# Reading q's and k's parts for attention as three runs each, twelve transfers a group in place of 18

## The reference

```python
h = _modulate(_ln(x), sh_msa, sc_msa)
qkv = (h @ w_qkv + b_qkv).reshape(B, N, 3, nh, hd).transpose(2, 0, 3, 1, 4)
q, k, v = (qkv[0], qkv[1], qkv[2])
attn = jax.nn.softmax(jnp.einsum('bhqd,bhkd->bhqk', q, k) * hd ** (-0.5), axis=-1)
o = jnp.einsum('bhqk,bhkd->bhqd', attn, v).transpose(0, 2, 1, 3).reshape(B, N, C)
x = x + g_msa[:, None, :] * (o @ w_proj + b_proj)
xn = _modulate(_ln(x), sh_mlp, sc_mlp)
x = x + g_mlp[:, None, :] * mlp(xn)
```

## Time and profile before

| | |
|---|---|
| median of three runs | 1612.34 us |
| the profiled execution: its time | 1615.5 us |
| the profiled execution: its span | 1613.7 us, 41194 instructions |
| TensorE matmuls busy | 1441.4 us, 89% |
| TensorE loads busy | 1082.4 us, 67% |
| VectorE busy | 1039.2 us, 64% |
| ScalarE busy | 780.9 us, 48% |
| GpSimd busy | 543.7 us, 34% |
| SyncE's transfers | 129.75 MB, 37.0% of 16 engines' span |

### The profile page before, as it was taken

How to read it: one execution, slowest core, us unless ns; L and a number is a source line. 1 busy time by engine, 2 the same in 40 slices (tenths; PEclk the granted TensorE clock), 3 DMA queues, 4 the chain that set the end, 5 groups by cost and what they waited for, 6 DMA issues and landing times. The chain is left out here.

```text
span 1613.7 us, 41194 instructions
## 1 busy us (share of the span) xinstructions
PE 1441.4 (89%) x15976; PEld 1082.4 (67%) x15976; DVE 1039.2 (64%) x2592; ACT 780.9 (48%) x1287; POOL 543.7 (34%) x739
## 2 busy tenths in 40 slices
PE   6789988999999998988999678787999798988998
PEld 2467666777777775766777467665776576666776
DVE  4678875666767666878447688886445565655342
ACT  2367654333323326766545366664544354645443
POOL 3345532211131303544334224433334243432321
PEclk9799999999999998999999789999999799988999
DMA  4765631111122214555011433443208576785021
GB/s 129 147 148 141 153 85 51 49 42 42 34 75 60 59 42 96 135 125 121 17 30 45 105 88 90 116 108 82 43 23 111 85 100 112 117 118 98 11 67 45
DMA packets 210858, 134.95 MB, mean 84 GB/s; under 512 B 144189, under 2 KB 193048, under 8 KB 204458
## 3 DMA queue, kind: packets, MB, share of 16 engines
q1 hardware_dynamic: 190706, 129.75, 37.0%
q10 hardware_dynamic: 19960, 2.57, 1.3%
HBM read 98.24 MB, written 33.24 MB: 81 GB/s over the span
## 5 line engine op out<-in xcount | busy, mean ns | idle before, releaser
L1532 DVE TENSOR_REDUCE negm<-banks 128x8 bf16<-128x1024 f32 x256 | 311.4, 1216 | 110.8 <-PE banks L650 108.4
L1223 ACT ACTIVATE prob<-banks 128x1024 f32<-128x1024 f32 x256 | 262.2, 1024 | 244.9 <-PE banks L672 244.2
L1949 POOL TENSOR_TENSOR X<-X,gx 128x288 f32<-128x288 f32 x128 | 104.9, 832 | 303.6 <-DVE gx L1562 301.7
L1350 ACT ACTIVATE hid<-banks 128x512 f32<-128x512 f32 x144 | 85.9, 597 | 230.5 <-PE banks L951 230.5
L650 PE MATMUL banks<-qk 54*128 54x128 bf16 (+1 forms) x2048 | 125.3, 245 | 65.5 <-DVE negm L1532 22.0
L668 PE MATMUL banks<-qk 54*128 54x128 bf16 (+1 forms) x2048 | 173.3, 239 | 8.6 <-ACT prob L1223 5.0
L967 PEld LDWEIGHTS banks<-wfc,hid 128*128 128x128 f32 x1152 | 156.6, 190 | 29.9 <-issue 19.9
L672 PE MATMUL banks<-mT,identb 64*128 64x128 bf16 x2048 | 170.2, 229 | 2.1 <-issue 2.1
L967 PE MATMUL banks<-wfc,hid 128*128 128x144 f32 x1152 | 161.1, 286 | 0.0
L950 PE MATMUL banks<-hT,wfc 128*128 128x512 f32 x288 | 149.4, 600 | 1.6 <-DMA wfc<-in_L_cond_w 1.1
L684 PE MATMUL banks<-prob,V 128*32 128x128 f32 x4096 | 150.5, 292 | 0.0
(11 more groups left out here) (165 smaller groups left out, 2822.8 us busy)
## 6 DMA issues: line engine op xcount, KB each, us to landing
qk<-qk_scr SPq DMA_DIRECT2D x336, 72.0 KB
gbuf<-gate_scr SPq DMA_DIRECT2D x64, 288.0 KB, 4.5
qk_scr<-parts SPq DMA_DIRECT2D x48, 288.0 KB, 3.0
qk<-qk_scr SPq DMA_DIRECT2D x48, 216.0 KB
qk<-cw_scr SPq DMA_DIRECT2D x8, 1024.0 KB, 4.6
qk<-tok_scr SPq DMA_DIRECT2D x112, 72.0 KB
qk_scr<-parts SPq DMA_DIRECT2D x48, 144.0 KB, 2.8
qk<-qk_scr SPq DMA_DIRECT2D x48, 144.0 KB
```

The lines of the kernel that those rows point to most:

```text
L1223: act.activation(prob[:, 2 * (U % 3):2 * (U % 3) + 2, :], pairs[1][:], ACT.Exp, scale=scale).then_inc(a_exp, 1)
L1532: dve.tensor_reduce(negm[:, u // 2, :, 4 * (u % 2):4 * (u % 2) + 4], pairs[0][:].rearrange("q s (h k) -> q s h k", k=T), AX.X, ALU.max, ne ...
L1949: pool.tensor_tensor(x, x, gx[:, q, :, :], ALU.add).then_inc(g_x, 1)
```

## The change

The six products are the same, in another order. q's blocks become 0, 1 | 0, 1, 2 | 0 and k's 0, 1, 2 | 0 | 0, 1, which pair as 00, 11, 02, 10, 20, 01. Each side is thus three runs of consecutive parts, and a run is one transfer: 18, 27 and 9 rows for q, and 27, 9 and 18 rows for k. `read_parts` issues 2 halves x 2 sides x 3 runs = 12 transfers a group in place of 18, in all four layers; `fetched` counts 96 for each third group. The rows, the bytes, the row lengths, the order of halves, the waits ahead of them and everything else stay as they are.

```diff
--- before.py
+++ after.py
@@ -26,6 +26,8 @@
 REM = 4 * CR_CH + 2
 QK_ROWS = 96
 QK_DIMS = QK_ROWS // H
+
+RUNS = (((0, 2), (0, 3), (0, 1)), ((0, 3), (0, 1), (0, 2)))
 KS = 6 * D
 TB = T // H
 TOK_V = [96, 48]
@@ -283,7 +285,7 @@
             return 64 * (n + 1) if n < 24 else 64 * 24 + 192 * (n + 1 - 24)
 
         def fetched(n):
-            return 144 * (n // 3 + 1)
+            return 96 * (n // 3 + 1)
 
         def normal(k):
 
@@ -430,22 +432,18 @@
                     sp.wait_ge(d_hg, CR + NT * (1 if n == 8 else 8))
                 sp.wait_ge(q_w, written(n))
                 for s in range(2):
-                    r0 = 64 * s
-                    for part in range(3):
-                        rows = (3 - part) * D
-                        if l < 3:
-                            q_src, k_src = (qk_scr[p, side, :, :, 8 * s:8 * s + 8].rearrange("a d h t -> (a d) (h t)")
-                                            for side in range(2))
-                            q_dst = qq[r0:r0 + rows, r].rearrange("r h t -> r (h t)")
-                            k_dst = kk[r0:r0 + rows, r].rearrange("r h t -> r (h t)")
-                        else:
-                            q_src, k_src = (tok_scr[p, side, 2 * s:2 * s + 2].rearrange("c b a d h w -> (a d) (c b) (h w)")
-                                            for side in range(2))
-                            q_dst, k_dst = qq[r0:r0 + rows, r], kk[r0:r0 + rows, r]
-                        sp.dma_start(q_dst, q_src[0:rows]).then_inc(q_r[r][s], 16)
-                        for i in range(3 - part):
-                            sp.dma_start(k_dst[D * i:D * i + D], k_src[D * part:D * part + D]).then_inc(q_r[r][s], 16)
-                        r0 += rows
+                    for side, runs in enumerate(RUNS):
+                        row = 64 * s
+                        for first, many in runs:
+                            if l < 3:
+                                src = qk_scr[p, side, first:first + many, :, 8 * s:8 * s + 8].rearrange("a d h t -> (a d) (h t)")
+                                dst = qk[row:row + many * D, side, r].rearrange("r h t -> r (h t)")
+                            else:
+                                src = tok_scr[p, side, 2 * s:2 * s + 2, :, first:first + many] \
+                                    .rearrange("c b a d h w -> (a d) (c b) (h w)")
+                                dst = qk[row:row + many * D, side, r]
+                            sp.dma_start(dst, src).then_inc(q_r[r][s], 16)
+                            row += many * D
 
             def turn_values(n):
                 sp.wait_ge(s_v, CR + 2 * n)
```

## The result

The changed kernel took 1569.62 us in the median of 4 runs (1562.78 to 1574.12), beside 1610.43 us (1606.91 to 1615.13) of the kernel before on the same chip: a ratio of 0.9736, 95% interval 0.9699 to 0.9773, 41 us less. The forecast was 1598.5 us with 1591 as its low end, so the sign was right and the size three times too small.

The account below looks back on a forecast made before the run. It took TensorE's waits for q's and k's reads, 41.0 us, as the most to gain, with nine DMA engines bounding each read. Layer gains of 5.1 + 4.9 + 2.1 + 1.7 = 13.8 us gave 1612.3 - 13.8 = 1598.5 us, range 1591 to 1613.

Parts of the forecast that it names:

- The last byte 1.7 us sooner: Reads of every group: fewer transfers bring the last byte 1.7 us sooner, with ends at nothing and 2.4 us.
- Nine engines as the bound: DMA reads of q and k: nine of 16 engines bound them from about first issue to last byte, share 0.57.
- SyncE's queue: I cost it at nothing: SyncE is through with a group's reads 2.4 us sooner; what stands behind them, writes included, was taken to gain nothing.
- The rule of neighbours, S(n) + S(n - 1): TensorE's waits for reads: the sum for two neighbouring groups stays fixed and falls by 1.7 us; layer 3 gains 5.1.
- The clock adds something I don't count: TensorE's matmuls after long waits run at the lower clock, eight taking 0.61 us or more against 0.40; counted at nothing.
- Issue or a fixed price sets the pace wholly: Rival on the reads: 2.4 us a group gained and a few clock stretches less, 1591 us; chance 0.06.
- The rows alone set the pace: Rival on the reads: the number of transfers doesn't matter, all 15 waits stay, 1612 us; chance 0.20.
- Slower by late instructions: Rival: reads posted faster delay instruction transfers, four more TensorE pauses at 5.5 us each, 1620 us; chance 0.12.
- The change doesn't do what it says: Rival: 27- and 18-row transfers into k's side would run on fewer engines than q's; given no chance of its own.

Follow-up runs that it names:

- the late start: Changed kernel with 60 satisfied waits on SyncE ahead of each group's first read, so every read starts later: 1599.5 us, ratio 0.9892.
- before, q first: Kernel before, own order of products and 18 transfers, but q's three runs issued first, then k's six blocks in ascending places: 1580.42 us.
- the sides in turn: Changed kernel's 12 transfers, with q's and k's runs issued alternately instead of q's three first: 1583.52 us, ratio 0.984.
- the cut into 14 and 13 rows: Changed kernel with each 27-row run cut into 14 and 13 rows, 16 transfers a group: 1577.85 us, ratio 0.9776.
- before, k out of place: Kernel before, 18 transfers, k's six blocks issued so that no block follows itself: 1629.79 us, ratio 1.0115.
- all single: Changed kernel with q's and k's runs all cut into nine-row blocks, 24 transfers a group: 1649.5 us, ratio 1.0265.
- 18 and 9: Changed kernel with each 27-row run cut into 18 and 9 rows, 16 transfers a group: 1588.86 us, ratio 0.9866.
- every sixth partition: The 24 nine-row transfers in the changed kernel's order, each block put on every sixth partition instead of neighbouring ones: 1697.64 us, ratio 1.0526.
- new order, k out of place: Changed kernel's order of products, 18 transfers, k's single blocks issued so that equal sources follow one another: 1625.3 us, ratio 1.0096.
- k in single blocks: Changed kernel with k's three runs cut into six nine-row blocks, 18 transfers a group: 1587.11 us, ratio 0.983.

## Why the forecast was wrong

**The last byte 1.7 us sooner: too small, and wrong in its reason.** The sum of 13.8 us is this term times some 8 us for each of its us. Both are too small, and they make the whole gap: measured were 2.6 us of landing and 16 us for each (the late start), that is some 42. The two reads on which the term rested drained 1.6 and 1.5 us sooner, and issuing fell to 4.23 us as said, so taken by the bytes alone the 1.7 looks right. But the forecast had seen that a group's reads land 18.0 us behind the first issue, where its own price of the bytes came to 13.7 and 14.9, and did not ask what the rest was; and it carried the price from layer 2 to layer 3, where the landing came 3.4 us sooner. Of the 2.6 us, 1.6 can be had by the order of issue alone (the kernel before, q first: 17.58 to 15.96), and 1.7 by fewer transfers with the sides in turn (to 15.87). The forecast cut each read into stretches of one kind and called the low rate of single blocks the price of a transfer. These blocks stood between transfers for the other side; six of them in a row, in place, behind q's runs, did better. No rival had "the order of issue matters", and the section on the change says that everything else stays as it is, though its diff puts all of a half's q transfers ahead of k's.

**Nine engines as the bound: not borne out.** It was read from a share of 0.57, since 9 of 16 are 0.56. By it the cut into 14 and 13 rows had to drain in 10.7 us; it took 13.6 and 13.9. It didn't spoil the sum, which was made from measured rates, but it was the ground on which everything else about the transfers was held fixed.

**"SyncE's queue: I cost it at nothing": wrong, in layer 3 above all.** The step named writes behind the reads, and took as cover that they come late anyway. The timeline of SyncE's queue in the kernel before shows otherwise. These are the twelve writes of groups 28 and 30, start and duration:

```profile
1344.08 15.87 SPq L416 DMA_DIRECT2D tok_scr<-parts  x12
...
1412.63 16.35 SPq L416 DMA_DIRECT2D tok_scr<-parts  x12
```

Group 27's reads were issued from 1333.01, and TensorE had them at 1351.04. The writes of group 28, begun at 1344.08, stood for 15.87 us until 1359.95. A single one of them took 5.99 us, up to 1350.43, that is until that read was nearly through; in group 30 one took 8.07:

```profile
1344.44 5.99 SPq L416 DMA_DIRECT2D tok_scr<-parts  x1
...
1413.00 8.07 SPq L416 DMA_DIRECT2D tok_scr<-parts  x1
```

Where writes began with the read ahead of them landed (groups 24, 26, 27, 29 and 31) the same twelve took 10.2 to 12.6. The changed kernel from group 27's read to group 31's, the writes of groups 28 to 31 and the reads of 27 to 31:

```profile
1300.08 5.74 SPq L445 DMA_DIRECT2D qk<-tok_scr  x12
...
1314.92 10.48 SPq L418 DMA_DIRECT2D tok_scr<-parts  x12
...
1328.87 6.20 SPq L445 DMA_DIRECT2D qk<-tok_scr  x12
1344.40 12.50 SPq L418 DMA_DIRECT2D tok_scr<-parts  x12
1360.11 5.61 SPq L445 DMA_DIRECT2D qk<-tok_scr  x12
1372.81 12.75 SPq L418 DMA_DIRECT2D tok_scr<-parts  x12
1388.95 7.46 SPq L445 DMA_DIRECT2D qk<-tok_scr  x12
1403.56 11.86 SPq L418 DMA_DIRECT2D tok_scr<-parts  x12
1418.61 6.22 SPq L445 DMA_DIRECT2D qk<-tok_scr  x12
```

Group 28's writes now take 10.48 us instead of 15.87, and group 30's 12.75 instead of 16.35. A read that is out of the way sooner pays twice: once for its own group, and once for the writes, and with them the read, of the next. For groups 28 to 31 the way from the first write to the landing fell by 5.6 us in the mean (35.6 to 30.0), 3.1 of them in the read. From group 24's first read to group 31's there were (1465.18 - 1224.72) / 7 = 34.4 us a group, and are (1418.61 - 1200.26) / 7 = 31.2. That is 3.2 us a group. That the writes queue behind the read is an inference from their times and durations; no run took the writes alone.

**The rule of neighbours, S(n) + S(n - 1), fixed but for 1.7: wrong in layer 3.** There the pairs fell by 6.9 (groups 27 and 28 together), 5.9 (29 with 28), 4.7 (30 with 29) and only 0.6 (31 with 30). The forecast kept 5.54 us for group 27 and 6.50 for 29, measured were 0 and 2.32. Group 31's 3.48 agrees with the 3.57 by accident. Its gain of 5.1 us had to be 13.7. The rule left out that the way itself, from parts to landing, passes through SyncE's queue. With the measured landing of each layer in place of 1.7, the same rule gives 10 us for layer 3 and some 21 in all; the waits fell by 13.7 and 25.8. In layers 0 to 2 the rule held better: group 2 to 1.48 (2.60), group 7 to 2.50 (3.13), group 23 to 3.19 (4.26), group 15 to 1.41 (0.54).

**"The clock adds something I don't count": the other mis-sized term.** Together with the pauses it is nearly half. Span differences from the changed kernel against the ledger:

| kernel | span | waits | pauses | at lower clock |
|---|---|---|---|---|
| changed | 1566.0 | 15.7 | 1.5 | 138 |
| before | +47.7 | +25.8 | +4.0 | +46 |
| late start | +28.7 | +17.5 | 0 | +28 |
| before, k out of place | +59.7 | +34.1 | +6.9 | +54 |
| all single | +78.7 | +54.1 | +1.5 | +66 |

What waits and pauses don't explain is 17.9, 11.2, 18.7 and 23.1 us: 0.39, 0.40, 0.35 and 0.35 us for each us at the lower clock. Four more traces give 0.40 (before, q first), 0.37 (18 and 9), 0.35 (every sixth partition) and 0.30 (new order, k out of place). It can't be over 0.5, what a TensorE busy throughout would lose between levels of 1.0 and 0.5. Close to the changed kernel the ledger is a few us off (k in single blocks: 21.4 us of span, of which waits and pauses explain 10.5, with 14 us more at the lower clock), so it is good for the large differences only. That the rest is the clock's is thus argued from how it goes with it, not tested. Read so, the 41 us of the medians (47.7 of the two spans) are by more than half waits for the reads, by a little under two fifths the low clock behind these waits, and the rest two pauses that went. The forecast had 13.8, 0 and 0. With 0.39 us per us at the lower clock, and 1.8 us of it for each us of wait (46 for 25.8), a us of wait on TensorE costs some 1.7 us of time in this kernel.

**The rivals.** *Issue or a fixed price sets the pace wholly* came nearest in time (1591) and is wrong in its first half: 7.77 us of issue changed nothing. Cutting the runs has a price; 24 transfers against 12 cost 80 us, in the direction of the Trainium skill's rule to coalesce (DMA: Bandwidth & Descriptors, section "Rules for kernel authors"), which the forecast had set aside since a group's landing contradicts 2 us in series. (The Trainium skill measured the 2 us on transfers issued by GpSimd, on the same page in the section "Anatomy of one DMA — SWDGE (gpsimd) path"; these are SyncE's.) *The rows alone set the pace* would have left all waits; they fell by 25.8 us. *Slower by late instructions*: one pause of 1.46 us in place of 2.14 and 3.29, and in the repeat of the changed kernel two, of 1.81 and 1.71; they neither grew in number nor went away for good, and no run here shows what they are. *The change doesn't do what it says*: it did, with shares of 0.51 to 0.59 as for q's runs before.

**What stays open.** Why alternating between q's and k's rows, and single blocks out of place, make the same transfers slower. Ruled out as the cause are the pace of issue, a source that is read again at once, the order of the products, and descending places with large transfers. Not separated are the two ends of a transfer: which rows of the scratch memory nine engines read at a time, and which partitions they write. Nor is it known what holds the reads at some 150 GB/s with 13 or 14 engines on them, when 177 and 178 were seen for short stretches with nine, nor why the nine were slower while others worked beside them.

## What to carry to other kernels

A busy share of DMA engines, even one that is just 9 of 16, doesn't show that they are the bound; compare the rates at the same share, and try a cut that brings more engines. When an edit turns the loops around a list of transfers, look at the order in which they are issued as at an edit of its own: here it gave three quarters of the gain by itself, and fewer transfers without it two thirds. Judge a read by when its semaphore says that it has landed, over all groups, and not by the bytes of two. And price a wait of TensorE with what hangs on it: the low clock behind it, and in a loop that goes through one queue, the writes of the next turn; moving the reads on purpose by a known time, as the late start did, gives that price in one run.

## What was unexpected of the hardware

- 18 transfers of the same bytes to the same rows took the kernel 1580, 1610 or 1630 us by the order in which SyncE issued them (landing after 15.96, 17.58 and 18.15 us).
- A DMA onto every second or sixth partition occupied SyncE for 0.73 us, one onto neighbouring partitions for 0.35; slow issue hidden behind the data cost nothing (10.17 us for 14, and the lowest median of all), and ruined the kernel where it wasn't (17.46 us for 24).
- The DMA engines' share went from 0.54 to 0.83 with 8% more bytes moved, and the whole read took no less time.
- A wait on a count already reached took SyncE 16, 25 and 31 ns in three kernels.
- A single write stood 5.99 and 8.07 us on SyncE while a read ahead of it was landing, against 0.5 to 1.1 us for most others.
